# Cross-attention over 16 sequences: row maxima in full 128-row tiles, queries turned for teams of sequences, stacks of three terms, and a new order in all five queues

## What is computed

```python
def layer0(x, ctx, mask):                 # 32 query heads, 8 key heads, head width 16
    q = (x @ Wq + bq).reshape(b, 100, 8, 4, 16).transpose(0, 2, 3, 1, 4)
    k = (ctx @ Wk + bk).reshape(b, 361, 8, 16).transpose(0, 2, 1, 3)
    v = (ctx @ Wv + bv).reshape(b, 361, 8, 16).transpose(0, 2, 1, 3)
    scores = einsum('bkgld,bksd->bkgls', q, k) / 4 + mask
    out = einsum('bkgls,bksd->bkgld', softmax(scores), v)
    return layernorm(out @ Wo + bo + x) * gamma + beta

def layer1(x1, ctx):                      # one head of width 512
    q, k, v = x1 @ w_q.T, ctx @ w_k.T, ctx @ w_v.T
    return x1 + alpha * (softmax(q @ k.T / sqrt(512)) @ v) @ w_o.T
```

## Time and profile before

| | |
|---|---|
| runs of the kernel | 667.99 us median of 3 (666.31 to 673.47) |
| span of the profiled execution | 672.3 us |
| PE busy | 643.7 us (96%) |
| DVE busy | 494.6 us (74%) |
| ACT and POOL busy | 396.1 and 397.9 us (59% each) |
| mean granted TensorE clock | 0.992 of full speed |
| DMA | 110.93 MB, queue of SP busy 59.4% of 16 engines' span |

### The profile page before, as it was taken

The page is one execution under the profiler, slowest core; times in us unless marked ns, Lnnn a source line. Parts: engine busy times, 40 slices in busy tenths (PEclk is TensorE's granted clock), DMA queues, the critical chain, the costliest instruction groups (busy, mean ns, idle before and its releaser), DMA issues.

```text
span 672.3 us, 11851 instructions
## 1 busy us (share of the span) xinstructions
PE 643.7 (96%) x3756; PEld 472.5 (70%) x3756; DVE 494.6 (74%) x1453; ACT 396.1 (59%) x588; POOL 397.9 (59%) x254
## 2 busy tenths in 40 slices
PE   3999899999999999999999999999999999999887
PEld 2656567777767878777777778787777777756454
DVE  2259488887778787878787878878787888785742
ACT  3314477766657666756766676766566656665321
POOL 7344568766465766667665657576666567563220
PEclk9999799999999999999999999999999999999999
DMA  8687564765574766767474747667675755443212
GB/s 290 226 185 213 127 174 136 194 187 126 145 238 110 229 155 195 165 183 194 137 215 128 238 106 240 135 200 172 189 175 158 203 138 151 121 101 117 88 45 71
DMA packets 47355, 110.93 MB, mean 165 GB/s; under 512 B 10095, under 2 KB 31663, under 8 KB 46783
## 3 DMA queue, kind: packets, MB, share of 16 engines
q1 hardware_dynamic: 47294, 110.19, 59.4%
HBM read 87.29 MB, written 22.46 MB: 163 GB/s over the span
## 4 chain that ended last, share of the span: by engine, by line
PE 75%; DMA 9%; issue 5%; POOL 4%; SPq 2%; DVE 2%; ACT 2%; POOLq 0%; DVEq 0%; ACTq 0%
PE mx_ps L750 11%; PE work L709 10%; PE work L710 10%; PE work L711 10%; PE o_ps L766 8%; PE work L823 6%; PE work L874 5%; PE sc_ps L737 3%; PE sc_ps L730 3%; PE sc_ps L738 3%; DMA qs<-mt_l 3%; PE work L779 3%; POOL pr L3948 2%; DMA k_dr<-k_l 2%; DMA qs<-q_dr 2%
## 5 line engine op out<-in xcount | busy, mean ns | idle before, releaser
L2406 DVE CUSTOM_DVE_ANT_0 mx_ps<-mx_ps,mask_n 100x361 f32<-100x361 f32 x512 | 271.6, 543 | 70.6 <-PE mx_ps L750 65.7
L3948 POOL TENSOR_TENSOR pr<-pr,mask_t 128x800 f32<-128x800 f32 x124 | 236.8, 1917 | 76.3 <-ACT pr L3252 75.9
L750 PE MATMUL mx_ps<-ks,qs 96*100 96x362 f32 x512 | 181.9, 369 | 0.9 <-DMA qs<-q_dr 0.6
L3259 ACT ACTIVATE pr<-pr 128x1200 f32<-128x1200 f32 x128 | 149.5, 1206 | 9.4 <-POOL pr L3948 5.4
L3252 ACT ACTIVATE pr<-sc_ps 128x800 f32<-128x800 f32 x124 | 104.0, 839 | 77.8 <-PE o_ps L766 51.0
L750 PEld LDWEIGHTS mx_ps<-ks,qs 96*100 96x100 f32 x512 | 84.4, 166 | 39.0 <-DVE mx L2406 11.3
L2392 DVE TENSOR_TENSOR pr<-sc_ps,mask_t 128x400 f32<-128x400 f32 x124 | 70.9, 572 | 24.6 <-PE sc_ps L730 14.3
L3960 POOL TENSOR_TENSOR c_l<-cT,c_h 128x1448 fp32r<-128x1448 f32 x16 | 53.4, 3338 | 51.4 <-ACT c_h L3284 51.4
L766 PE MATMUL o_ps<-pr,va 128*32 128x400 f32 (+1 forms) x768 | 73.0, 514 | 0.0
L2406 DVE DVE_READ_ACCUMULATOR2_ANT mx<- 100x1 f32 x512 | 72.3, 141 | 0.0
L823 PEld LDWEIGHTS work<-late 128*128 128x128 f32 (+1 forms) x384 | 49.7, 191 | 7.0 <-issue 5.9
(11 more groups left out here) (163 smaller groups left out, 1223.4 us busy)
## 6 DMA issues: line engine op xcount, KB each, us to landing
qs<-q_dr SPq DMA_DIRECT2D x64, 200.0 KB, 4.3
ks<-k_dr SPq DMA_DIRECT2D x128, 96.0 KB, 3.7
late<-in_ctx SPq DMA_DIRECT2D x16, 768.0 KB, 7.2
cT<-in_ctxT SPq DMA_DIRECT2D x16, 724.0 KB, 5.4
late<-in_ctxT SPq DMA_DIRECT2D x16, 724.0 KB, 6.0
o_dr<-o_s SPq DMA_DIRECT2D x30, 200.0 KB, 3.5
xT<-in_xT SPq DMA_DIRECT2D x16, 200.0 KB, 3.9
q_dr<-q_h SPq DMA_DIRECT2D x16, 200.0 KB
```

What stands on the lines that cost most here:

```text
L750: nc.tensor.matmul(mx_ps[0:L, n % 2, 0:SP2], qs[p][0:TERMS, g, L * j:L * (j + 1)], ks[p][0:TERMS, g, 0:SP2], start=True, stop=True).then_i ...
L2406: V.tensor_tensor_reduce(out=src, in0=src, in1=mask_n[p][:, :], scale=1.0, scalar=-3.0e38, op0=ALU.add, op1=ALU.max, accum_out=mx[p][:, n: ...
L3259: A.activation(t, t, ACT.Exp).then_inc(ex_ok, 1)
L3948: G.tensor_tensor(t, t, mask_t[p][:, 1:3, :].unsqueeze(2).to_broadcast([P, 2, J, L]), ALU.add).then_inc(sc_pool, 1)
```

## The change

- **Maxima in full tiles.** The 8 x 400 query columns of a sequence are cut into tiles of 128: 24 tiles of one key head each, and one tile of what is left over (16 columns of each of the 8 heads), which POOL gathers into a zero-padded tile `rest` (`rests`) and PE computes with four matmuls. So 25 tiles are computed and reduced where 32 heads were. The mask for these tiles is 128 x 4 x 361, held once and loaded in three pieces (`mask_in(b, c)`).
- **Rows of maxima through memory.** After 13 and 25 tiles the maxima are turned, split, written to memory (`maxima_out`) and read back as rows (`maxima_in`). That is a second DMA in a row, behind a wait for the first.
- **Turned queries for teams.** The six teams are sequences (0, 1), (2, 3, 4), (5, 6, 7), (8, 9, 10), (11, 12, 13) and (14, 15). The weights are now the stationary operand, so the queries come out turned. A team takes 48 matmuls of 300 (or 200) columns. `turn_q`, `row_n` and their DVE step are gone; ACT adds the bias as it makes the high part.
- **Stacks of three terms.** Two key heads share one stack of 96 rows, 48 for each (high-high, high-low, low-high), and the queries have zeros where the other head's rows are. `ks` is half as wide. Three parts are written to memory for each of q and k, and read back with 6 DMAs a sequence, not 12.
- **No fillers.** The 36 matmuls without a reader are gone.
- **Order.** All five queues have a new order, in which one stretch is no longer like the next.

```diff
-            def heads(b, n0, n1):
-                    wait(pe, a_mx, NH * b + n - 1)
-                    nc.tensor.matmul(mx_ps[0:L, n % 2, 0:SP2], qs[p][0:TERMS, g, L * j:L * (j + 1)],
-                                     ks[p][0:TERMS, g, 0:SP2], start=True, stop=True).then_inc(a_mm, 1)
+            def tiles(b, n0, n1):
+                    c, g = tile_of(n)
+                    if n == HALF_TILES - 1:
+                        pe.wait_ge(rest_ok, b + 1)
+                    wait(pe, a_mx, at - 1)
+                    if g is None:
+                        for r in range(PAIRS):
+                            w = 96 * (r + 1)
+                            mm = nc.tensor.matmul(dst, rest_flat[:, w:w + P], ks[p][0:TERMS, r, 0:SP2],
+                                                  start=(r == 0), stop=(r == PAIRS - 1))
+                    else:
+                        mm = nc.tensor.matmul(dst, qs[p][0:TERMS, g, P * c:P * (c + 1)], ks[p][0:TERMS, g // 2, 0:SP2],
+                                              start=True, stop=True)
...
             def maxima_in(b, half):
-                wait(sp, mh_ok[half], b + 1)
-                wait(sp, ml_ok[half], b + 1)
-                for row, t in ((TERMS, mt_h[half]), (TERMS + 1, mt_l[half])):
-                    sp.dma_start(dst, t[:, :].bitcast(F32)).then_inc(m_in[half], 16)
+                sp.wait_ge(m_out[half], 16 * (b + 1))
+                sp.dma_start(qs[p][TERMS:ROWS, gs, 0:SC * P].bitcast(F32),
+                             m_dr[b, half, :, first:first + 4 * SC, :].rearrange("t (g c) r -> t g (c r)", c=SC)
+                             ).then_inc(m_in[half], 16)
+                sp.dma_start(qs[p][TERMS:ROWS, gs, SC * P:JL].bitcast(F32),
+                             m_dr[b, half, :, last, 64 * half:64 * half + 64].rearrange("t (g r) -> t g r", g=4)
+                             ).then_inc(m_in[half], 16)
+            def maxima_out(b, half):
+                wait(sp, mh_ok[half], b + 1)
+                wait(sp, ml_ok[half], b + 1)
+                sp.dma_start(m_dr[b, half, :, :, :].rearrange("t n r -> n t r"),
+                             mt[half].bitcast(F32)).then_inc(m_out[half], 16)
...
-            def q_part(b, k0, k1):
-                    mm = product(work[0:L, 1, :], x_h[:, xs], x_l[:, xs], wq_h[:, k, :], wq_l[:, k, :], k, KT - 1)
+            def q_part(t, j, k0, k1):
+                n = len(TEAMS[t])
+                    mm = product(work[:, 1, 0:n * L], wq_h[:, k, js], wq_l[:, k, js],
+                                 x_h[:, k, 0:n, :].rearrange("p i l -> p (i l)"),
+                                 x_l[:, k, 0:n, :].rearrange("p i l -> p (i l)"), k, KT - 1)
...
+            def rests(b):
+                for half in range(2):
+                    pool.wait_ge(st_in[half][p], 48 * (b // 2 + 1))
+                G.tensor_copy(rest[:, :, 96:P].rearrange("k r (t i) -> k r t i", t=2),
+                              qs[p][0:TERMS, :, SC * P:JL].bitcast(F32).rearrange("k (r t) i -> k r t i", t=2)
+                              ).then_inc(rest_ok, 1)
```

More of the change, by code:

```diff
@@ L962, in keep_busy @@
-            def keep_busy(count, free, value):
-                pe.wait_ge(free, value)
-                dst = sc_ps[0:L, 2, :] if free is fl_ok and value == 3 else o_ps[0:L, :]
-                for _ in range(count):
-                    nc.tensor.matmul(dst, wk_h[:, 0, 0:L], wq_h[:, 0, :], start=True, stop=True)
-            q_part(0, 0, 4)
+            k_part(0, 0, 2)
             fold_m(0, 0, 1)
-            turn_q(0)
+            k_part(0, 2, 4)
+            fold_m(3, 0, 1)
+            v_part(0, 0, 1)
@@ L1138, in _ @@
-            k_part(3, 2, 3)
-            heads(2, 14, 15)
-            scores(1, 5, 0, 1)
-            k_part(3, 3, 4)
-            heads(2, 15, 16)
+            v_part(3, 2, 4)
+            tiles(1, 22, 23)
+            scores(1, 2, 0, 1)
+            tiles(1, 23, 24)
+            scores(1, 2, 1, 3)
+            tiles(1, 24, 25)
+            tiles(2, 0, 1)
+            scores(1, 3, 1, 3)
+            tiles(2, 1, 2)
+            turn_maxima(1, 1)
+            tiles(2, 2, 3)
+            scores(1, 3, 0, 1)
@@ L1147, in _ @@
+            turn_maxima(2, 0)
             scores(1, 7, 1, 3)
[L1148 to L1157 removed]
+            k_part(4, 0, 1)
+            tiles(2, 16, 18)
+            k_part(4, 1, 2)
+            scores(1, 7, 0, 1)
+            tiles(2, 18, 19)
@@ L1158, in _ @@
+            k_part(4, 2, 4)
+            tiles(2, 19, 23)
+            values(1, 1)
+            tiles(2, 23, 25)
+            y_part(0, 0, 2)
+            scores(2, 0, 0, 1)
+            turn_maxima(2, 1)
+            tiles(3, 0, 1)
+            scores(2, 0, 1, 3)
             y_part(0, 2, 3)
-            heads(2, 23, 24)
+            tiles(3, 1, 2)
+            turn_v(3)
             y_part(0, 3, 4)
-            v_part(3, 1, 2)
-            heads(2, 24, 25)
-            scores(2, 0, 0, 1)
-            heads(2, 25, 26)
@@ L1398, in _ @@
             scores(4, 6, 1, 3)
-            d_part(2, 1, 2)
-            heads(5, 15, 16)
+            v_part(6, 0, 1)
+            tiles(5, 11, 13)
+            d_part(2, 0, 2)
+            tiles(5, 13, 14)
             d_part(2, 2, 3)
@@ new lines, in _ @@
+            tiles(6, 4, 5)
+            s1_part(3, 2, 4)
+            scores(5, 3, 0, 1)
+            scores(5, 3, 1, 3)
+            tiles(6, 5, 7)
+            v_part(7, 1, 3)
+            turn_p1(3)
+            v_part(7, 3, 4)
+            tiles(6, 7, 9)
+            cx_part(3, 0, 2)
+            scores(5, 4, 0, 1)
+            tiles(6, 9, 10)
+            scores(5, 4, 1, 3)
+            tiles(6, 10, 11)
+            cx_part(3, 2, 4)
+            tiles(6, 11, 12)
+            values(5, 0)
+            tiles(6, 12, 13)
```

3986 lines of the change are left out of this document (1858 added, 2128 removed).

## The result

The changed kernel takes 676.76 us (median of 5, 674.61 to 683.52); the kernel before has 668.42 beside it. The ratio is 1.0127, with a 95% interval of 1.0087 to 1.0166: 1.3% slower where 3% faster was forecast. Two of the ten runs of e4 and one of the ten of e12 were over 1.5% above the fastest of their kernel and are left out of medians and ratios; the profile of e4 is of one of these.

The account below looks back on a forecast made before the run. PE was taken as the bound in the steady part: 672.3 - 31.5 (shorter list) + 6 (start) - 1.7 + 3 (hand-off) + 2 (end) = 650.1 us, less 4.3 for the median: 646 us. Own range 638 to 654, wider range 632 to 664.

Parts of the forecast that it names:

- What bounds the kernel: Steady part, eight sequences: PE waits for nobody, so each microsecond off its list is gained; 294.3 us to near 280.
- Maxima and queries: PE's maxima and query matmuls: 10.6 and 12.5 us less; DVE's reductions 77 us less, its busy time about 410.
- the rival of 664 us: "No gain": 288 query matmuls each wait out a whole weight load, so 18 us of gain go; chance 0.06.
- Fillers: Removing 36 unread matmuls from PE: worth between nothing and 8.4 us, counted as 8.4 us of gain.
- the stretch forecast at 49 us: From 63.4 to 122.0 us, 58.6 us long before: 49 taken, 1.7 us of gain beyond PE's shorter list.
- the 3.5 us beside the rival: Clock price in the partly-eaten rival (654 to 662 us, chance 0.16): without fillers, stretches with waits run slower, 3.5 us.
- Start: Before the first scores: PE begins near 11 us, 6 us more waiting (3 to 9), first scores near 72 us.
- Hand-off: Maxima through memory, then back to PE as rows: need 6.2 us with a 2.3 us write, 3 us of waiting counted.
- The table of room: PE's time between `turn_maxima` and the scores: 7 of 32 short at 6.2 us need, 20 by 33 us at 8.3.
- the paragraph on what costs nothing: POOL gathers, ACT and DVE query steps, mask loads and SP issues: counted as free, on engines over 30% idle.
- Falls below 0.9 in a stretch: Sign that the forecast is wrong: granted clock below 0.9 in a stretch behind sequence 2.
- Slower: Rival: the maxima's write takes 4.4 us, need 8.3, 20 hand-offs short, 30 us more than counted: 676 us; chance 0.07 or 0.08.

Follow-up runs that it names:

- e4: The kernel before without its 36 fill matmuls: 670.74 us, ratio 1.0008 to the kernel before.
- e12: The changed kernel itself, unaltered, run again in a later series: 676.75 us, ratio 1.008 to the kernel before.
- e8: e7 with ten unread 512-column matmuls put on PE into waits for DVE between the second and third sequence: 655.05 us, ratio 0.9783.
- e1: The changed kernel with POOL waiting after each `deviation` until `shift` is done: 662.07 us, ratio 0.9878 to the kernel before.
- e7: e1 with another start: context split first, second context's low part on DVE, fold products in front of waits: 658.95 us, ratio 0.984.
- e3: e1 with maxima first written to a second memory buffer, lengthening each of the 32 hand-offs: 669.67 us.
- e5: The kernel before with ten small unused POOL additions directly behind `deviation` of sequences 3 to 9: 673.17 us, ratio 1.0061.
- e2: The changed kernel with 8, 24 and 18 unread matmuls on PE before the waits for `x` of sequences 0, 1 and 7: 675.15 us.

## Why the prediction was wrong

The forecast was 646 us with a range of 632 to 664; it came out at 676.8. Step by step:

**What bounds the kernel: right.** Where PE waits for nobody, the shorter list came back. With the holds gone, eight steady sequences took 282.0 us (e8), forecast 280, before 294.3.

**Maxima and queries: right.** 384 + 64 matmuls, 0.170 us apart (forecast 0.166); query products 0.138 to 0.140 and 0.112 us apart (0.14 and 0.11). A weight load bounds nothing here; the rival of 664 us is out. DVE, 442.7 us busy where 410 was forecast, has 14 us of holds in it (428.3 without them, e1). The other 18 are a mis-sized term: summed, DVE's durations fell by 82 us (589.5 to 507.3), near the 85 forecast, but they overlap (the 0.14 us that reads a maximum ends beside the next instruction), and busy time fell by 66. It costs nothing where PE is the bound.

**Fillers: wrong by 8.4 us.** The prediction had written that their going is worth between nothing and 8.4 us, and then took the upper end. e4 measured the lower one: in the kernel before they stood in waits, and these grew when they went. 6 of the 8.4 us belonged to the stretch forecast at 49 us, which took 55.5 in the change and 53.4 in e8. That they were paid for by a clock kept up (the 3.5 us beside the rival) e4 doesn't show: its clock was low for only 3.4 us more. Put back in the changed kernel, ten of them won about 1.3 us (e8).

**Start: the size was wrong.** PE began at 11.2 us, as said, though behind `wk_l`, itself held until 11.1 us, and not behind the low part of the context, done at 10.55. The wait for `c_low(1)` was 3.4 us against 3.5 forecast. But the first scores came at 80.5, not 72. The query round trip that I counted at 2.5 us cost nothing; what I did not count were waits of 1.4 us behind `k_part(1)` and 1.0 behind the first query product, where the next product needs the one PSUM bank that ACT and DVE have to empty first, with fold products placed between parts that needed no cover. e7 put them in the gaps: 74.6 us. Part of the delay is not lost time: PE is busy for 59.96 us ahead of the first scores where it was for 51.42, with work that now stands earlier (237 matmuls against 186).

**Hand-off: no cost.** 3 us were counted, none was measured. The landing of the way out, 1.7 us, was below the 2.3 taken. The table of room behind it was too pessimistic as well: it gave 30 us more for 2 us more of need, and e3 paid 7.6. Probably because it summed PE's list by prices, while PE meets other waits on its way, in which the hand-off runs on; the runs don't show that by itself. The fixed 2 us of a DMA, cited from the Trainium skill, decided nothing; the measured 1.7 is a little under it (the section named is on DMAs that GpSimd issues, here SP does).

**The step that failed: 13.2 us.** It is the paragraph on what costs nothing. No part of the prediction looked at what the new order puts beside `centre` and `shift`. What it costed at nothing it costed by busy shares ("on engines with over 30% idle in the steady part"); what counts is which instruction runs beside which. The Trainium skill has the rule, in "SBUF — State Buffer", section "SBUF: two separate sides": VectorE and GpSimd share one pair of SBUF ports as an exclusive lock, and a VectorE operation with two SBUF inputs and a GpSimd operation that reads SBUF block each other, and whoever starts first keeps it. The traces agree, 0.75 us of `shift` becoming 1.46 beside one POOL addition of 1.03 us. They add that the hold goes on through an unbroken run of POOL instructions (6.54 us for `deviation` and three additions) and ends in the first gap (0.82 in e5). The kernel before shows the rule too, the other way round, and it could have been read there. DVE's timeline, then POOL's:

```profile
309.42 0.75 DVE L2493 SCALAR_TENSOR_TENSOR y<-y,mv,gamma_b 100x512 f32<-100x512 f32 x1
```

```profile
309.46 1.13 POOL L3971 TENSOR_TENSOR rstd<-ve,half_c 100x1 f32<-100x1 f32 x1
```

`centre`, begun 0.04 us ahead, takes its 0.75 us, and `deviation` takes 1.13 instead of 0.57. So it is in 8 of the 16 sequences. `centre` and `shift` were never held there: `shift` always began before POOL's next instruction, and at the start `wk_l` (11.25, 0.69 us) was done before `c_low` began at 12.60.

**Clock.** Behind its cold start it was at its lower level for 34 us in the changed kernel's profile, in five stretches, and for 10 us in that of the kernel before. "Falls below 0.9 in a stretch" was a sign that the forecast is wrong. Between 136.0 and 224.5 us it was 0.90, at the edge, and in the shorter windows shown it was 0.61 to 0.69. The cause of three of the five falls was the wait for the layer norm and not, as the rival had it, the hand-off; they are gone in e1. On the price of one fall, by pairs of profiles: 1.0 and 2.7 us (e2 against e12), 1.3 us (e8 against e7).

**The sum again,** on the scale of medians. 645.8, plus 8.4 (fillers), less 3 (hand-off), is 651.2; e8 took 655.05. The 3.9 us between them stay open (the kernel before took 670.96 us in e8's series and 668.42 beside the result, which may be 2.5 of them). From e8 to e1 it is 7.0 us (start, fillers and what e8 was ahead without them), and from e1 to the changed kernel 14.7, or 13.2 within one series: the holds and the falls of the clock behind them. That is 676.8.

**Chances.** "Slower" had 0.07, all of it on the hand-off. That its rival named 676 us is chance: the need of 8.3 us behind this number never arose, and e3 paid 7.6 us for 1.7 more in every hand-off, not 30. The rivals were all drawn from what the diff names. The one that came lay between two engines neither of which was changed in what it computes there.

## To carry to other kernels

When an order is rewritten, list for each vector instruction with two SBUF inputs what GpSimd may now be doing beside it, above all right behind the step that releases the vector instruction; a held 0.75 us instruction can cost 6 us, and one wait on the engine with time to spare mends it. Before counting removed fillers as gain, look at whether they stand in front of a wait: if they do, they are worth nothing gone, and perhaps something where they are. Judge a new wait by the room that a trace shows, and look for the wait that the diff does not name in the instructions whose length changed.

## What the hardware did that was not expected

- `centre` and `shift`, 0.75 us alone, took 1.46 us beside one POOL addition, 2.04 beside one mask addition, 2.98 beside `deviation` and one, 5.57 beside `c_low` and one, 6.54 beside `deviation` and three. `wk_l` at the start took 2.60 us beside `c_low` (before: 0.69) and ended although a POOL memset followed at once. Each of these six ended 0.55 us behind the end of POOL's run. Beside `deviation` alone `centre` kept its 0.75 us, even where `deviation` had begun 0.09 us ahead (sequence 2 of the changed kernel).
- DVE's reduction of the maxima (L2204), with one input in PSUM, did not suffer: its longest of 400 is 0.58 us, with POOL busy beside more than half of them.
- `deviation` on POOL, 0.57 us alone, took 1.13 us beside a `centre` that had begun 0.04 to 0.05 us ahead of it, in 8 sequences of the kernel before; in a ninth, also 0.04 us apart, both kept their usual time (0.77 and 0.57).
- After PE's waits for `shift` of 1.5, 6.0 and 4.3 us the granted clock was at its lower level for 7 to 10 us; in another execution of the same kernel (e12), where the wait of sequence 0 was 0.7 us, it kept 2.4 GHz there.
